# A first layer norm without a mean: centred embedding weights, squares summed on ScalarE

## The chip, the cores and the metric

The kernel runs on one core of one Trainium2 chip. The metric is the device time of one execution in microseconds (us). Of the kernel before there are three timed runs: 1298.17, 1299.24 and 1303.66 us, median 1299.24 us. The engines are called PE (TensorE), ACT (ScalarE), DVE (VectorE), POOL (GpSimd) and SP (the queue that starts most transfers).

## The reference

The model is an audio tower: patches of the signal are embedded and normalised, one attention layer follows, then a feed-forward layer in which each token picks 2 of 6 experts.

```
x: (128, 1000, 16)
patches = x[:, starts[:, None] + arange(16), :]      # stride 8: 124 tokens of 256 values
y   = einsum('bpi,di->bpd', patches, W) + b          # W 256 x 256
mu  = mean(y, axis=-1);  var = mean(square(y - mu), axis=-1)
h   = (y - mu) * rsqrt(var + 1e-5) * gamma + beta    # the first layer norm
h   = h + attention(layernorm(h))                    # one head of width 256, per batch item
h   = h + experts(layernorm(h))                      # router, softmax, top 2 of 6, 3-layer MLP each
```

The outputs are 128 x 124 tokens of 256 values in float32.

## The kernel before, in words

The kernel has two phases. The **first phase** takes 4 batch items (a group of 4 x 124 tokens) at a time, 32 groups in all, through a software pipeline. Every iteration `it` runs seven stages, each on another group: stage -2 splits the group's x into a rounded high part and a low part (`xT_hi` on ACT, `xT_lo` on DVE), stage -1 embeds it, stage 0 finishes the first layer norm and makes the second, stages 1 and 2 do attention, stages 3 and 4 the router, the choice of experts and the place of each token in its expert's list; stage 5 only sends the last rows. The loop runs `it` from -2 to 35. The **second phase** runs 67 tiles of 512 rows through the expert layers; two or three of its tiles are started between the last iterations of the first.

There is no scheduler: the order in which each engine takes its instructions is the order in which the code of its block is written, and engines wait for one another by counting semaphores. An instruction that waits holds back all that stands behind it on its engine. The semaphore `ln1` counts DVE's steps of one group in the first two layer norms (`LN1_N` of them), and `wait_apart` is a wait as an instruction of its own.

In stage -1 PE multiplies the group's patches by the embedding weights into banks 6 and 7 of PSUM, two batch items (a pair) per bank. The weights `proj_raw["tok"]` and the bias `bias_raw["tok"]` are split once at the start, high on ACT (`high_halves`, `high_bias`) and low on DVE (`low_halves`, `low_bias`). The product for the next group may overwrite a bank when DVE has made `y` from it (`bank_read`).

The steps that the change touches:

- DVE, stage -1, `statistics(0, ...)` (the line of `bn_stats` is L1030, that of `bn_aggr` L1033): for each of the four items a `bn_stats` over the 256 values of each token in PSUM, then an aggregation into mean and variance, `mv`.
- POOL, `inverse_std(0, ...)` (L499, L502): `rstd` of the group from the variance in `mv`. The same function serves the other two layer norms. Between its calls POOL issues eight indirect transfers (L510), which send each token's row to its experts' lists.
- DVE, stage -1, L1175: `y = (embedded - mean) * gamma`, four instructions, each of 256 columns.
- DVE, stage 0, L1098: `h = y * rstd + beta`; `statistics(1, ...)` for the second layer norm.
- ACT has no step between `xT_hi` (L905) and `qT` (L912).

Other names below: `half_w` (ACT L932, DVE L1143) is the splitting of the experts' weights, one piece of 256 columns in each iteration from 4 to 27 and three in each of 0 to 3; `nmr` (L1148, L1071) is minus mean times rstd of the second and third layer norm; `hav`, the residual sum behind attention, is L1161; `lshift` (L1235) is the router's logits less their maximum, which ACT's `pexp` (L858) reads; `rec` (L877) is the third layer norm's output, which PE transposes (L665); `xn` (L940) is the second's, transposed in L615.

Of the kernel before, what the change touches and what calls it, by code (L numbers as in the profile page):

```python
# [24 lines left out]
ALU = mybir.AluOpType  # L25
ACT = mybir.ActivationFunctionType
AX_X = mybir.AxisListType.X
# [34 lines left out]

LN1_N, AV_N, TOPK_N, POS_N = 25, 14, 25, 4
ADDED = 16 * TB
# [23 lines left out]
def audio_tower(nc, x, tok_w, tok_b, tok_gamma, tok_beta, wq, bq, wk, bk, wv, bv, scale,  # L88
                rw1, rb1, rw2, rb2, eweights, esmall, out):
    with ExitStack() as ctx:  # L90
# [36 lines left out]
        stats = sb("stats", [P, 3, GB, 6])  # L127
        mv = sb("mv", [P, 3, GB, 2])
        vareps = sb("vareps", [P, 3, GB])
        rstd = sb("rstd", [P, 3, GB])  # L130
# [42 lines left out]
        with ExitStack() as part_a:  # L173
# [30 lines left out]
        S = {n: sem(n) for n in (  # L204
            "tok_loaded", "const_loaded", "pool_const", "dve_const", "invs", "proj_high", "proj_low", "bias_zero",
            "w_high", "w_low", "dummy_cleared", "xT_high", "xT_low", "xn1T_low", "tok_ps", "ln1", "rstd1", "rstd2", "rstd3", "xn1_ready", "xn1T_ps", "xn1T_sb",
# [255 lines left out]
        def _(pool):  # L462
# [34 lines left out]
            def inverse_std(which, ready, g):  # L497

                pool.tensor_scalar(vareps[0:TOK, which, :], mv[0:TOK, which, :, 1], EPS, None,  # L499
                                   ALU.add).then_inc(ready, 1)  # L500
                pool.wait_ge(ready, g * 2 + 1)
                pool.tensor_tensor(rstd[0:TOK, which, :], vareps[0:TOK, which, :], neghalf[0:TOK, :],  # L502
                                   ALU.pow).then_inc(ready, 1)
# [10 lines left out]
            def step(it, group_of):  # L514
                xa, x0, x2, x4, x5 = (group_of(s) for s in (-1, 0, 2, 4, 5))
                if x0:
                    g, slot, rnd = x0
                    wait(pool, S["xn1_ready"], g * GB)
                    wait_apart(pool, S["ln1"], g * LN1_N + 6 * GB, S["pool_passed"])
                    inverse_std(1, S["rstd2"], g)  # L520
                if x5:
                    scatter(x5[0], range(5, 7))
                if xa:
                    g, slot, rnd = xa
                    wait_apart(pool, S["ln1"], g * LN1_N + 2 * GB, S["pool_passed"])
                    inverse_std(0, S["rstd1"], g)
                if x5:
                    scatter(x5[0], range(7, 8))
                if x2:
                    g, slot, rnd = x2  # L530
                    wait(pool, S["xn2_ready"], g * GB)
# [35 lines left out]
        def _(pe):  # L567
# [37 lines left out]
            def step(it, group_of):  # L605
# [21 lines left out]
                if it == DRAIN - 2:  # L627
                    pe.wait_ge(S["ln1"], (G - 1) * LN1_N + 3 * GB)
                    turn(0, 6)
# [8 lines left out]
                if xa:  # L638
                    g, slot, rnd = xa
                    pe.wait_ge(S["xT_high"], g + 1)  # L640
                    pe.wait_ge(S["xT_low"], g + 1)
                    if it == -1:
                        pe.wait_ge(S["proj_low"], 2)
                    for pair in range(2):
                        bank_read(pe, (S["ln1"], g - 1, (g - 1) * LN1_N + 2 * GB + 2 + 2 * pair))
                        for j in (0, 1):
                            at = (2 * pair + j) * ROWS_X
                            into = banks[6 + pair][0:TOK, j * D:(j + 1) * D]
                            for c in range(DC):
# [176 lines left out]
        def _(act):  # L826
# [20 lines left out]

            act.wait_ge(S["tok_loaded"], N_TOK)
            act.wait_ge(S["pool_const"], 2)
            high_halves("tok")  # L850
            high_bias("tok")

            def step(it, group_of):
                xs, x0, x1, x2, x3, x4 = (group_of(s) for s in (-2, 0, 1, 2, 3, 4))
                if x4:
# [44 lines left out]
                if xs:  # L900
# [3 lines left out]
                    wait(act, S["xT_low"], g)  # L904
                    act.activation(xT_hi[:], x_in[:, slot, :], ACT.Identity).then_inc(S["xT_high"], 1)  # L905
                if x1:
                    g, slot, rnd = x1
# [93 lines left out]
        def _(v):  # L1001
# [10 lines left out]

            v.wait_ge(S["tok_loaded"], N_TOK)
            v.wait_ge(S["pool_const"], 16)
# [3 lines left out]

            def embedded(j):

                return banks[6 + j // 2][R, (j % 2) * D:(j % 2 + 1) * D]

            def statistics(which, src, s, at, g):

                for j in range(GB):
                    if which == 0:
                        v.wait_ge(S["tok_ps"], g * 2 + j // 2 + 1)
                    else:
                        v.wait_ge(s, at - GB + 1 + j)
                    v.bn_stats(stats[R, which, j, :], src(j)).then_inc(s, 1)  # L1030
# [33 lines left out]
            def step(it, group_of):  # L1064
# [25 lines left out]
                if x0:  # L1090
# [5 lines left out]
                    for j in range(GB):  # L1096
                        v.wait_ge(S["ln1"], at + 2 * GB + 1 + j)
                        v.scalar_tensor_tensor(out=h[R, g % KEPT, j, :], in0=y[R, j, :], scalar=rstd[R, 0, j:j + 1],  # L1098
                                               in1=beta_bc[R, :], op0=ALU.mult, op1=ALU.add).then_inc(S["ln1"], 1)
                if x0:  # L1100
                    g, slot, rnd = x0
                    statistics(1, lambda j: h[R, g % KEPT, j, :], S["ln1"], g * LN1_N + 4 * GB, g)
                if x4:
# [46 lines left out]
                if it == DRAIN - 2:  # L1150
                    rows_low(0)
                if xa:
                    g, slot, rnd = xa
                    statistics(0, lambda j: embedded(j), S["ln1"], g * LN1_N, g)
                if x2:
# [270 lines left out]
```

## Time and profile before

| | |
|---|---|
| median of three timed runs | 1299.24 us |
| profiled execution: its own time, its span | 1298.97 us, 1297.2 us |
| PE, busy | 1222.9 us (94%) |
| PE weight loads, busy | 1075.9 us (83%) |
| DVE, busy | 1060.5 us (82%) |
| POOL, busy | 918.8 us (71%) |
| ACT, busy | 843.3 us (65%) |
| mean granted clock of PE | 0.984 |

The span is the time from the first to the last instruction; 1.8 us of the execution's own time lie around it. The shares are means over both phases. The first phase fills roughly the first 600 us, the second the rest, and the engines' shares differ between them. A row of the timeline gives start, duration (of a merged run of several instructions: from the first's start to the last's end), engine, line, operation, output and inputs, count, and in brackets how long the engine had been idle and what released it. Instructions of one engine overlap a little, so the distance from start to start is shorter than the duration.

### The profile page before, as it was taken

The page shows a single profiled execution, that of the slowest core. Times are in us where ns is not written, and L with a number is a line of the kernel's source. Part 1 is how long each engine was busy: PE and PEld are TensorE (multiplying, and loading weights), DVE is VectorE, ACT ScalarE, POOL GpSimd, SP SyncE. Part 2 cuts the span into 40 slices and gives each one's busy share as a digit, 9 for nine tenths or more (in the row PEclk, how much of TensorE's full clock was granted, in tenths as well). Part 3 has the DMA queues.
Part 4 walks back from the last instruction along what each step waited for, and adds up shares of the span by engine and source line. Part 5 has one row for each costly group of instructions (what it writes and reads, how often), then busy time and mean ns, then how long its engine had stood idle before and what let it go on. Part 6 is the DMA issues. An engine that isn't in the chain of part 4 may idle for free. (4 is left out here: it accounts for less than half of the span.)

```text
span 1297.2 us, 28243 instructions
## 1 busy us (share of the span) xinstructions
PE 1222.9 (94%) x7888; PEld 1075.9 (83%) x7888; DVE 1060.5 (82%) x3593; ACT 843.3 (65%) x1838; POOL 918.8 (71%) x740
## 2 busy tenths in 40 slices
PE   4999999999999999999898999999999999999993
PEld 4888888888888888888677888888888888889883
DVE  5789999999999999998777778777777777878783
ACT  2677677667667757776655667676666666666662
POOL 2127777877777777787788777777676767767776
PEclk8899999999999999999999999999999999999997
DMA  4224555544444444554469989766696687687745
GB/s 133 83 85 126 146 144 150 138 116 115 120 118 115 126 112 109 156 167 123 118 182 203 255 188 234 134 114 127 112 236 108 125 193 154 108 185 164 128 55 60
DMA packets 137193, 180.45 MB, mean 139 GB/s; under 512 B 38345, under 2 KB 103501, under 8 KB 137037
## 3 DMA queue, kind: packets, MB, share of 16 engines
q0 software_dynamic: 75456, 69.19, 32.9%
q1 hardware_dynamic: 60316, 108.67, 27.5%
q8 instruction: 64, 1.05, 0.3%
q10 hardware_dynamic: 1264, 0.79, 0.2%
q14 instruction: 93, 0.75, 0.2%
HBM read 159.01 MB, written 101.49 MB: 201 GB/s over the span
## 5 line engine op out<-in xcount | busy, mean ns | idle before, releaser
L559 POOL DMA_INDIRECT out<-yo,tail x268 | 434.2, 1620 | 168.8 <-issue 138.1
L510 POOL DMA_INDIRECT expert_rows<-rec,row_i x256 | 354.7, 1386 | 72.6 <-issue 59.4
L979 ACT ACTIVATE h2v<-bank,small 128x512 f32<-128x512 f32 x134 | 92.3, 690 | 204.6 <-PE bank L777 203.3
L804 PE MATMUL bank<-w_sb,h_hi 128*128 128x256 f32 x1072 | 208.8, 288 | 4.1 <-issue 3.6
L777 PE MATMUL bank<-x_hi,w_sb 128*128 128x512 f32 x536 | 178.6, 395 | 5.7 <-DVE x_lo L1337 4.8
L777 PE MATMUL bank<-h_hi,w_sb 128*128 128x512 f32 x536 | 177.4, 392 | 1.4 <-issue 1.4
L804 PEld LDWEIGHTS bank<-w_sb,h_hi 128*128 128x128 f32 x1072 | 171.6, 191 | 4.9 <-issue 4.2
L804 PE MATMUL bank<-w_sb,h_lo 128*128 128x256 f32 x536 | 151.7, 283 | 0.0
L777 PEld LDWEIGHTS bank<-x_hi,w_sb 128*128 128x128 f32 x536 | 101.8, 190 | 27.5 <-issue 5.0
L777 PEld LDWEIGHTS bank<-h_hi,w_sb 128*128 128x128 f32 x536 | 101.0, 188 | 21.4 <-issue 1.7
L985 ACT ACTIVATE yo<-yo,gcol 128x256 f32<-128x256 f32 x268 | 113.9, 498 | 4.7 <-DVE yo L1368 4.7
L573 PE MATMUL bank<-tok_proj,xT_hi 128*124 128x256 f32 x512 | 103.0, 294 | 13.6 <-DVE xT_lo L1139 9.4
L1352 DVE CAST h_hi<-h1v 128x512 fp32r<-128x512 f32 x134 | 62.4, 466 | 64.5 <-ACT h1v L972 64.5
L499 POOL TENSOR_SCALAR vareps<-mv 124x4 f32<-124x4 f32 x96 | 23.1, 241 | 123.5 <-issue 65.1
L502 POOL TENSOR_TENSOR rstd<-vareps,neghalf 124x4 f32<-124x4 f32 x96 | 102.4, 1067 | 8.0
L777 PE MATMUL bank<-x_lo,w_sb 128*128 128x512 f32 x268 | 105.4, 393 | 0.0
L777 PE MATMUL bank<-h_lo,w_sb 128*128 128x512 f32 x268 | 105.2, 392 | 0.0
L804 PEld LDWEIGHTS bank<-w_sb,h_lo 128*128 128x128 f32 x536 | 102.9, 192 | 0.0
L1352 DVE CAST h_hi<-h2v 128x512 fp32r<-128x512 f32 x134 | 58.1, 434 | 49.7 <-ACT h2v L979 49.4
L1337 DVE TENSOR_TENSOR h_lo<-h1v,h_hi 128x512 fp32r<-128x512 f32 x134 | 93.2, 695 | 4.6
L1337 DVE TENSOR_TENSOR h_lo<-h2v,h_hi 128x512 fp32r<-128x512 f32 x134 | 93.1, 694 | 4.6
L573 PE MATMUL bank<-v_proj,xn1T_hi 128*124 128x256 f32 x512 | 94.5, 285 | 0.0
(190 smaller groups left out, 3113.3 us busy)
## 6 DMA issues: line engine op xcount, KB each, us to landing
w_sb<-split_weights SPq DMA_DIRECT2D x189, 512.0 KB
xg<-expert_rows SPq DMA_DIRECT2D x67, 530.0 KB, 4.7
out<-h SPq DMA_DIRECT2D x32, 496.0 KB
split_weights<-half_w SPq DMA_DIRECT2D x36, 256.0 KB, 4.1
small<-in_esmall SPq DMA_DIRECT2D x67, 134.0 KB
x_in<-in_x SPq DMA_DIRECT2D x32, 250.0 KB, 10.7
expert_rows<-pad_rows SPq DMA_DIRECT2D x9, 530.0 KB, 9.1
raw_w<-in_eweights SPq DMA_DIRECT2D x36, 128.0 KB, 4.1
```

The source lines that it names most:

```text
L499: pool.tensor_scalar(vareps[0:TOK, which, :], mv[0:TOK, which, :, 1], EPS, None, ALU.add).then_inc(ready, 1)
L502: pool.tensor_tensor(rstd[0:TOK, which, :], vareps[0:TOK, which, :], neghalf[0:TOK, :], ALU.pow).then_inc(ready, 1)
L510: pool.indirect_dma_start(rows_dram, bass.IndirectOffsetOnAxis(ap=row_i[0:TOK, slot, j, k:k + 1], axis=0), rec[0:TOK, slot, j, :], None).t ...
L559: pool.indirect_dma_start(out, bass.IndirectOffsetOnAxis(ap=tail[:, t % TAILS, j, E8:].bitcast(I32), axis=0), yo[:, t % YO, j, :], None, c ...
L573: mm = pe.matmul(bank, lhs[a], rhs[b], start=(first and n == 0), stop=(last and n == 2))
L777: mm = pe.matmul(banks[bank + m][:], w[:, n, c, wh, m * P:(m + 1) * P], act[:, c, :], start=(c == 0 and p == 0), stop=(c == DC - 1 and p = ...
L804: mm = pe.matmul(banks[6 + b][:, (j % 2) * D:(j % 2 + 1) * D], act[:, c, j * P:(j + 1) * P], w[:, 2, c, wh, :], start=(c == 0 and p == 0), ...
L979: act.activation(h2v[:, m, :], banks[bank + m][:], ACT.Relu, bias=small[:, t % SLOTS, DC + m:DC + m + 1]).then_inc(S["h2_v"], 1)
L985: act.activation(yo[:, t % YO, j, :], yo[:, t % YO, j, :], ACT.Identity, scale=gcol[:, t % YO, j:j + 1]).then_inc(S["y_gated"], 1)
L1337: v.tensor_tensor(lo, val, hi.bitcast(F32), ALU.subtract).then_inc(ready, 1)
L1352: v.tensor_copy(hi[:, m, :], val[:, m, :]).then_inc(s, 1)
```

## The change

The embedding weights and the bias are made free of their mean over the 256 outputs, once, at the start, by DVE (`centre`). What PE then puts into PSUM has mean zero for each token, up to rounding. The mean is no longer computed or subtracted; the variance is the mean of the squares. ACT squares each item's 256 values from PSUM and lets the accumulator sum them into `sumsq`; POOL takes the variance from there. DVE's four `bn_stats` and four aggregations of the first layer norm go, and `y` is made by two instructions of 512 columns instead of four of 256. ACT's split of the embedding weights waits for `centre`.

```diff
-LN1_N, AV_N, TOPK_N, POS_N = 25, 14, 25, 4
+LN1_N, AV_N, TOPK_N, POS_N = 15, 14, 25, 4
...
             def inverse_std(which, ready, g):
-                pool.tensor_scalar(vareps[0:TOK, which, :], mv[0:TOK, which, :, 1], EPS, None,
-                                   ALU.add).then_inc(ready, 1)
+                if which == 0:
+                    pool.tensor_scalar(vareps[0:TOK, which, :], sumsq[0:TOK, :], 1.0 / D, EPS, ALU.mult,
+                                       ALU.add).then_inc(ready, 1)
+                else:
+                    pool.tensor_scalar(vareps[0:TOK, which, :], mv[0:TOK, which, :, 1], EPS, None,
+                                       ALU.add).then_inc(ready, 1)
...
                 if xa:
                     g, slot, rnd = xa
-                    wait_apart(pool, S["ln1"], g * LN1_N + 2 * GB, S["pool_passed"])
+                    wait_apart(pool, S["squares"], (g + 1) * GB, S["pool_passed"])
                     inverse_std(0, S["rstd1"], g)
...
-                        bank_read(pe, (S["ln1"], g - 1, (g - 1) * LN1_N + 2 * GB + 2 + 2 * pair))
+                        bank_read(pe, (S["ln1"], g - 1, (g - 1) * LN1_N + 1 + pair))
...
-            act.wait_ge(S["tok_loaded"], N_TOK)
+            act.wait_ge(S["centred"], 4)
             act.wait_ge(S["pool_const"], 2)
             high_halves("tok")
+            act.wait_ge(S["centred"], 10)
             high_bias("tok")
...
+                if xa:
+                    g, slot, rnd = xa
+                    wait(act, S["rstd1"], g * 2)
+                    for j in range(GB):
+                        act.wait_ge(S["tok_ps"], g * 2 + j // 2 + 1)
+                        wait(act, S["squares"], g * GB + j)
+                        act.activation(square[0:TOK, :], banks[6 + j // 2][0:TOK, (j % 2) * D:(j % 2 + 1) * D], ACT.Square,
+                                       accum_out=sumsq[0:TOK, j:j + 1]).then_inc(S["squares"], 1)
...
+            def centre():
+
+                s = S["centred"]
+                v.wait_ge(S["tok_loaded"], N_TOK)
+                v.tensor_reduce(tok_mean[:], proj_raw["tok"][:], AX_X, ALU.add).then_inc(s, 1)
+                v.wait_ge(s, 1)
+                v.tensor_scalar(tok_mean[:], tok_mean[:], 1.0 / D, None, ALU.mult).then_inc(s, 1)
+                v.wait_ge(s, 2)
+                for c in range(DC):
+                    v.tensor_scalar(proj_raw["tok"][:, c, :], proj_raw["tok"][:, c, :], tok_mean[:, c:c + 1], None,
+                                    ALU.subtract).then_inc(s, 1)
...
+            centre()
             v.wait_ge(S["pool_const"], 16)
             low_halves("tok", 1)
             low_bias("tok", 3)
...
-                if xa:
-                    g, slot, rnd = xa
-                    statistics(0, lambda j: embedded(j), S["ln1"], g * LN1_N, g)
...
-                    for j in range(GB):
-                        v.wait_ge(S["ln1"], at + GB + 1 + j)
-                        v.scalar_tensor_tensor(out=y[R, j, :], in0=embedded(j), scalar=mv[R, 0, j, 0:1],
-                                               in1=gamma_bc[R, :], op0=ALU.subtract, op1=ALU.mult).then_inc(S["ln1"], 1)
+                    for pair in range(2):
+                        v.wait_ge(S["squares"], g * GB + 2 * pair + 2)
+                        v.tensor_tensor(y[R, 2 * pair:2 * pair + 2, :],
+                                        banks[6 + pair][R, :].rearrange("p (b n) -> p b n", b=2),
+                                        gamma_bc[R, :].unsqueeze(1).to_broadcast([TOK, 2, D]), ALU.mult
+                                        ).then_inc(S["ln1"], 1)
```

The part left out of `centre` does the same with the bias: for its copies in partitions 0 and 32 a sum over the 256 values, a product with 1/256 and a subtraction.

DVE, from the weights' split to the router's shift, in one steady iteration before:

```order
L1143 TENSOR_TENSOR half_w<-raw_w,half_w 128x256
L1148 SCALAR_TENSOR_TENSOR nmr<-mv,rstd 124x4
L1030 BN_STATS stats<-bank 124x6 x4
L1033 BN_AGGR mv<-stats 124x2 x4
L1161 SCALAR_TENSOR_TENSOR h<-bank,rinv,h 124x256 x4
L1030 BN_STATS stats<-h 124x6 x4
L1033 BN_AGGR mv<-stats 124x2 x4
L1175 SCALAR_TENSOR_TENSOR y<-bank,mv,gamma_bc 124x256 x4
L1230 TENSOR_TENSOR logits<-bank,rb_bc 124x4x6
L1233 TENSOR_REDUCE lmax<-logits 124x4
L1235 TENSOR_TENSOR lshift<-logits,lmax 124x32
```

The same stretch of DVE now:

```order
L1173 TENSOR_TENSOR half_w<-raw_w,half_w 128x256
L1178 SCALAR_TENSOR_TENSOR nmr<-mv,rstd 124x4
L1188 SCALAR_TENSOR_TENSOR h<-bank,rinv,h 124x256 x4
L1060 BN_STATS stats<-h 124x6 x4
L1063 BN_AGGR mv<-stats 124x2 x4
L1202 TENSOR_TENSOR y<-bank,gamma_bc 124x512 x2
L1259 TENSOR_TENSOR logits<-bank,rb_bc 124x4x6
L1262 TENSOR_REDUCE lmax<-logits 124x4
L1264 TENSOR_TENSOR lshift<-logits,lmax 124x32
```

The statistics of the bank are gone, and `h`, which reads PE's attention output, follows `nmr` at once; `y` is two instructions.

ACT, from the router's exponential on, in one steady iteration before:

```order
L858 ACTIVATE pexp<-lshift 124x32
L866 ACTIVATE xn1T<-bank,ones_r 128x496 x2
L870 ACTIVATE xn1T_hi<-xn1T 128x496 x2
L877 ACTIVATE rec<-h,nmr,rstd 124x256 x4
L886 ACTIVATE probs<-bank,negmax 124x124 x4
L893 ACTIVATE xn2T<-bank 128x496 x2
L899 ACTIVATE gexp<-gap 124x4
L905 ACTIVATE xT_hi<-x_in 128x500
L912 ACTIVATE qT<-bank,score_col 128x496 x2
L917 ACTIVATE pT<-bank 125x496
L921 ACTIVATE rhT<-bank,rb_col 128x496
L932 ACTIVATE half_w<-raw_w 128x256
```

The same stretch of ACT now:

```order
L866 ACTIVATE pexp<-lshift 124x32
L874 ACTIVATE xn1T<-bank,ones_r 128x496 x2
L878 ACTIVATE xn1T_hi<-xn1T 128x496 x2
L885 ACTIVATE rec<-h,nmr,rstd 124x256 x4
L894 ACTIVATE probs<-bank,negmax 124x124 x4
L901 ACTIVATE xn2T<-bank 128x496 x2
L907 ACTIVATE gexp<-gap 124x4
L913 ACTIVATE xT_hi<-x_in 128x500
L920 ACTIVATE square,sumsq<-bank 124x256 x4
L928 ACTIVATE qT<-bank,score_col 128x496 x2
L933 ACTIVATE pT<-bank 125x496
L937 ACTIVATE rhT<-bank,rb_col 128x496
```

Four squares stand between `xT_hi` and `qT`, ahead of `pT`, `rhT` and `half_w`. On PE nothing moves; on POOL the second `rstd` of an iteration waits for `squares` instead of `ln1`.

## Rows read from the trace of the kernel before

**Rows 1.** One iteration: length, busy PE, PEld, DVE, ACT, POOL (instructions), clock, DMA.
```profile
309.90:328.90 19.00, 18.31 (x130) 15.95 (x129) 17.39 (x79) 13.32 (x32) 14.92 (x15) 1.00 0.45 118
```
**Rows 2.** Timeline of DVE: `negmax` of the iterations 4 and 28.
```profile
85.74 0.67 DVE L1076 TENSOR_REDUCE negmax<-bank 124x4 f32<-124x496 f32 x1
...
543.81 0.67 DVE L1076 TENSOR_REDUCE negmax<-bank 124x4 f32<-124x496 f32 x1
```
**Rows 3.** Timeline of DVE, second half of one iteration.
```profile
323.87 0.43 DVE L1143 TENSOR_TENSOR half_w<-raw_w,half_w 128x256 fp32r<-128x256 f32 x1 [0.57 <-ACT half_w L932]
...
324.28 1.42 DVE L1030 BATCH_NORM_STATS2 stats<-bank 124x6 f32<-124x256 f32 x4
...
325.97 1.66 DVE L1161 SCALAR_TENSOR_TENSOR h<-bank,rinv,h 124x256 f32<-124x256 f32 x4
...
329.18 1.63 DVE L1175 SCALAR_TENSOR_TENSOR y<-bank,mv,gamma_bc 124x256 f32<-124x256 f32 x4
330.73 0.17 DVE L1230 TENSOR_TENSOR logits<-bank,rb_bc 124x24 f32<-124x24 f32 x1
...
331.15 0.19 DVE L1235 TENSOR_TENSOR lshift<-logits,lmax 124x32 f32<-124x32 f32 x1
```
**Rows 4.** Timeline of ACT, from `pexp` of that iteration to its `rhT`.
```profile
312.39 0.23 ACT L858 ACTIVATE pexp<-lshift 124x32 f32<-124x32 f32 x1 [2.51 <-DVE lshift L1235]
312.52 1.22 ACT L866 ACTIVATE xn1T<-bank,ones_r 128x496 f32<-128x496 f32 x2
...
321.19 0.58 ACT L917 ACTIVATE pT<-bank 125x496 f32<-125x496 f32 x1 [0.27 <-PE bank L700]
322.86 0.67 ACT L921 ACTIVATE rhT<-bank,rb_col 128x496 f32<-128x496 f32 x1 [1.09 <-PE bank L708]
```
**Rows 5.** Timeline of PE in the same iteration.
```profile
314.86 0.28 PE L652 MATMUL bank<-tok_bias,ones_r 128*124 128x256 f32 x1
315.39 0.73 PE L665 MATMUL bank<-ident,rec 124*128 124x124 f32 x2 [0.26 <-ACT rec L877]
...
317.28 0.47 PE L573 MATMUL bank<-xn1T_hi,q_proj 128*128 128x496 f32 x1
...
322.65 1.89 PE L722 MATMUL bank<-v_sb,pT 125*124 125x256 f32 x8
...
328.08 1.01 PE L615 MATMUL bank<-ident,xn 124*128 124x124 f32 x8
```
**Rows 6.** Timeline of POOL: the same transfer in two iterations that follow one another.
```profile
552.50 1.43 POOL L510 DMA_INDIRECT expert_rows<-rec,row_i  x1 [0.24 <-issue]
...
570.09 1.43 POOL L510 DMA_INDIRECT expert_rows<-rec,row_i  x1 [0.24 <-issue]
```
**Rows 7.** Timeline of ACT: `probs`, with the read of its accumulator.
```profile
297.63 0.35 ACT L886 ACTIVATE probs<-bank,negmax 124x124 f32<-124x124 f32 x1
297.87 0.20 ACT L886 ACTIVATION_READ_ACCUMULATOR probs<-bank,negmax 124x1 f32 x1
297.97 0.35 ACT L886 ACTIVATE probs<-bank,negmax 124x124 f32<-124x124 f32 x1
```
**Rows 8.** Groups by line; columns: count | busy us, mean ns | idle before.
```profile
L1368 DVE TENSOR_TENSOR yo<-bank,small 128x512 f32<-128x512 f32 x134 | 85.8, 681 | 2.2 <-PE bank L804 2.2
...
L940 ACT ACTIVATE xn<-h,nmr,rstd 124x256 f32<-124x256 f32 x128 | 66.4, 590 | 18.2 <-DVE nmr L1148 18.2
...
L952 ACT ACTIVATE v_sb<-bank 124x512 f32<-124x512 f32 x64 | 37.9, 596 | 38.8 <-PE bank L573 38.8
...
L932 ACT ACTIVATE half_w<-raw_w 128x256 fp32r<-128x256 f32 x36 | 13.8, 407 | 0.0
...
L840 ACT ACT_TABLE_LOAD x1 | 1.3, 1283 | 4.4 <-POOL pad_rows L489 4.4
...
L1039 DVE TENSOR_REDUCE key_sum<-bank 128x2 f32<-128x512 f32 x1 | 0.7, 674 | 0.0
```
**Rows 9.** Timeline of DVE: its first instruction.
```profile
7.18 0.69 DVE L1005 TENSOR_TENSOR tok_proj<-tok_raw,tok_proj 128x512 fp32r<-128x512 f32 x1 [7.18 <-ACT tok_proj L840]
```

More of the change, by code:

```diff
@@ L128, in audio_tower @@
         mv = sb("mv", [P, 3, GB, 2])
+        square = sb("square", [P, D])
+        sumsq = sb("sumsq", [P, GB])
+        tok_mean, bias_mean = sb("tok_mean", [P, DC]), sb("bias_mean", [P, 1])
         vareps = sb("vareps", [P, 3, GB])
@@ L204, in audio_tower @@
         S = {n: sem(n) for n in (
-            "tok_loaded", "const_loaded", "pool_const", "dve_const", "invs", "proj_high", "proj_low", "bias_zero",
+            "tok_loaded", "const_loaded", "centred", "squares", "pool_const", "dve_const", "invs", "proj_high", "proj_low", "bias_zero",
             "w_high", "w_low", "dummy_cleared", "xT_high", "xT_low", "xn1T_low", "tok_ps", "ln1", "rstd1", "rstd2", "rstd3", "xn1_ready", "xn1T_ps", "xn1T_sb",
@@ L518, in step @@
                     wait(pool, S["xn1_ready"], g * GB)
-                    wait_apart(pool, S["ln1"], g * LN1_N + 6 * GB, S["pool_passed"])
+                    wait_apart(pool, S["ln1"], g * LN1_N + 2 + 3 * GB, S["pool_passed"])
                     inverse_std(1, S["rstd2"], g)
@@ L627, in step @@
                 if it == DRAIN - 2:
-                    pe.wait_ge(S["ln1"], (G - 1) * LN1_N + 3 * GB)
+                    pe.wait_ge(S["ln1"], (G - 1) * LN1_N + 2)
                     turn(0, 6)
@@ L846, in high_bias @@
                                    ).then_inc(S["proj_high"], 1)
-            act.wait_ge(S["tok_loaded"], N_TOK)
+            act.wait_ge(S["centred"], 4)
             act.wait_ge(S["pool_const"], 2)
             high_halves("tok")
+            act.wait_ge(S["centred"], 10)
             high_bias("tok")
             def step(it, group_of):
-                xs, x0, x1, x2, x3, x4 = (group_of(s) for s in (-2, 0, 1, 2, 3, 4))
+                xs, xa, x0, x1, x2, x3, x4 = (group_of(s) for s in range(-2, DEPTH))
                 if x4:
@@ L1011, in low_bias @@
                                 ALU.subtract).then_inc(S["proj_low"], 1)
-            v.wait_ge(S["tok_loaded"], N_TOK)
+            def centre():
[8 more added lines that the diff above has]
+                                    ALU.subtract).then_inc(s, 1)
+                for r in (0, 32):
+                    v.tensor_reduce(bias_mean[r:r + 1, :], bias_raw["tok"][r:r + 1, :], AX_X, ALU.add).then_inc(s, 1)
+                v.wait_ge(s, 6)
+                for r in (0, 32):
+                    v.tensor_scalar(bias_mean[r:r + 1, :], bias_mean[r:r + 1, :], 1.0 / D, None, ALU.mult).then_inc(s, 1)
+                v.wait_ge(s, 8)
+                for r in (0, 32):
+                    v.tensor_scalar(bias_raw["tok"][r:r + 1, :], bias_raw["tok"][r:r + 1, :], bias_mean[r:r + 1, 0:1], None,
+                                    ALU.subtract).then_inc(s, 1)
+            centre()
             v.wait_ge(S["pool_const"], 16)
@@ L1017, in _ @@
             R = slice(0, TOK)
-            def embedded(j):
-                return banks[6 + j // 2][R, (j % 2) * D:(j % 2 + 1) * D]
             def statistics(which, src, s, at, g):
                 for j in range(GB):
[L1026 to L1029, printed above, removed]
+                    v.wait_ge(s, at - GB + 1 + j)
                     v.bn_stats(stats[R, which, j, :], src(j)).then_inc(s, 1)
@@ L1096, in step @@
                     for j in range(GB):
-                        v.wait_ge(S["ln1"], at + 2 * GB + 1 + j)
+                        v.wait_ge(S["ln1"], at + 1 + j // 2)
                         v.scalar_tensor_tensor(out=h[R, g % KEPT, j, :], in0=y[R, j, :], scalar=rstd[R, 0, j:j + 1],
@@ L1101, in step @@
                     g, slot, rnd = x0
-                    statistics(1, lambda j: h[R, g % KEPT, j, :], S["ln1"], g * LN1_N + 4 * GB, g)
+                    statistics(1, lambda j: h[R, g % KEPT, j, :], S["ln1"], g * LN1_N + 2 + GB, g)
                 if x4:
```

## Prediction, made before the changed kernel ran

> **What bounds the kernel now.** I read the busy time by stretch first, then the timelines of the engines through one iteration, then the single forms. The change touches only the first phase and the start, so the second phase is taken as it is.
>
> One steady iteration of the first phase takes 19.0 us; in it PE is busy for 18.3, DVE 17.4, POOL 14.9 and ACT 13.3 us, at a full granted clock [rows 1]. The `negmax` of iterations 4 and 28 stand 458.07 us apart, 24 iterations of 19.09 us; 2.1 us of these are extras, 1.7 of them the choice of the early expert in one iteration [rows 2]. No busy share says which engine sets the 19.0 us, so I followed the waits round one turn:
>
> - DVE waits 0.57 us for ACT's `half_w` at 323.87 us and then runs until `lshift` ends at 331.34 us: 7.47 us [rows 3].
> - `lshift` releases ACT's `pexp`, for which ACT had idled 2.51 us. From `pexp` at 312.39 us ACT goes through its list to the `half_w` that releases DVE at 323.87 us: 11.48 us. Within them ACT idles 0.27 us ahead of `pT` and 1.09 ahead of `rhT`, for PE [rows 3, 4].
>
> 7.47 + 11.48 + 0.03 for the handover = 18.98 us: this ring is the bound, DVE for two fifths of it, then ACT and PE.
>
> Just below it lie the engines alone. PE idles 0.41 us ahead of its transposes of `rec` (314.86 + 0.12 to 315.39 us), which then take 1.89 us, paced by ACT, where eight of the same form in L615 take 1.01 us to the last end, some 0.85 to the next start: 19.0 - 0.41 - 1.04 = 17.55 us [rows 5]. POOL, where it waits for nobody, needs 17.59 us for a turn [rows 6]. DVE, less its 0.57 us and some 0.5 of smaller waits, needs about 17.9.
>
> **The change, part by part.**
>
> *DVE, the statistics.* From the bank's `bn_stats` at 324.28 us to L1161 at 325.97 us: 1.69 us go [rows 3]. They lie on the ring.
>
> *DVE, `y`.* Four instructions take 1.55 us from start to start (329.18 to 330.73 us) [rows 3]. The two new ones have the form of L1368, 512 columns from a bank with a broadcast operand, 0.68 us each [rows 8]; start to start some 0.61. 1.55 - 1.22 = 0.33 us go, also on the ring. It would be 0.19 if they did not overlap.
>
> *ACT, four squares.* The trace has no square. A plain pass over 512 columns of a bank takes 0.596 us, a plain one over 256 columns of SBUF 0.407 [rows 8]; I take 0.42 for 256 from a bank. The accumulator's read follows: in `probs` it begins 0.24 us after the start of a 0.35 us pass, lasts 0.20 and so ends 0.09 us behind it [rows 7]. Each square waits for the one before, with another 0.03: 0.42 + 0.09 + 0.03 = 0.54, say 0.53 us each and 2.1 us for the four. Lower bound: `probs` repeats every 0.34 us [rows 7] and 132 more columns add 0.11: 0.45, in all 1.8. Upper bound: as slow as L940's 0.590 us pass with two pointer operands [rows 8] and the same 0.12: 0.71, in all 2.8.
>
> The page "ScalarE: Activation LUTs" of the Trainium skill, section "What ACT_TABLE_LOAD costs", gives a pass with immediate operands as 186 ns plus 0.833 ns per column, 399 ns here, and 93 ns for each pointer operand; L932's 407 ns and L940's 590 ns agree. By it a square is 0.52 us, the four 2.1; with a pointer as bias it would be 0.61 and 2.45.
>
> On the ring the squares stand ahead of `pT` and `rhT`. They first fill the 1.36 us for which ACT idles there, and lengthen ACT's part only by 2.1 - 1.36 = 0.74 us.
>
> *The new ring.* 18.98 - 1.69 - 0.33 + 0.74 = 17.7 us. A second one comes up beside it. ACT from `xn1T` at 312.52 to the end of `pT` at 321.77 us is 9.25 us, less the 0.27 idle, plus the squares: 11.1 us. The late `pT` holds back PE's L722, and from there (322.65 us) to the end of the transposes of `xn` (329.09 us) are 6.44 us, upon which ACT's `xn1T` waits: 17.5 us [rows 4, 5]. With PE's 17.55 and POOL's 17.59 four limits lie within 0.2 us. I take 17.75 us for the iteration, a little above the highest.
>
> *POOL.* Its `rstd1` will find the squares done long before (they end some 9 us behind `pexp`), so that one wait goes. It was not on the ring. In iterations 28 to 30, where there is no `half_w`, the period is set by DVE alone before (17.6 to 17.9) and by the second ring now: no gain.
>
> *What is queued behind the new waits.* Behind the squares on ACT stand `qT`, `pT`, `rhT` and `half_w`, and PE and DVE wait for these; this is counted above. DVE's `y` waits for the squares, which end some 7 us before its turn. Its `h` (L1161) now comes 1.69 us earlier after `nmr`, but DVE's 0.57 us wait for `half_w` grows to about 1.4, so it arrives when PE's product is there.
>
> *The start.* DVE's first work was at 7.18 us, behind ACT's split [rows 9]. Now `centre` comes ahead of ACT: a reduction over 512 columns (0.67 us as L1039 [rows 8]), a small product, two subtractions; then the bias, four passes over 256 columns of one partition and two small ones. That is 3 to 4 us of DVE, partly beside ACT's split; PE's first product starts about 2.6 us later. In the first iterations PE's product, two squares and `y` form a chain, 1.1 us of squares in place of 1.7 of statistics, while three `half_w` stand behind the squares. I count +2 us until iteration 3 (bounds 0 and +4).
>
> **The sum.** 24 iterations of 17.75 us are 426.0 us. Of the 2.1 us of extras I leave 1.0, since the longer wait of DVE at `half_w` covers part of the early choice: 427. 458.07 - 427 = 31 us saved. Iteration 3 to 4 gives 1 more, the start costs 2: 30 us. The execution profiled took 1298.97 us, which is 0.3 below the median, so no correction: 1298.97 - 30 = **1269 us**. Its own range goes by the squares: at 1.8 us the other limits hold 17.6, saving 33 to 34; at 2.45 the ring is 18.1, saving some 22: 1264 to 1278.
>
> **The rivals.**
>
> *ACT takes the ring over.* Squares at 2.8 us make 18.4 us an iteration: 24 x 0.6 = 14 us saved and 1 from the extras, less the start: about 1285. For it: four serial steps, each with an accumulator read, on the engine whose slack ahead of `pT` is only 1.36 us. Against it: ACT is busy 13.3 of 19 us and the forms nearest are short. The page named above says in "Rules for kernel authors" that plain multiplications belong on VectorE rather than on ScalarE, which speaks against this move; the row of L932 against the 1.69 us on DVE shows that ACT's price is higher, 2.1 against 1.7, but paid in idle time.
>
> *PE is the bound already.* If its 18.31 busy of 19.0 us could not be compressed, an iteration would stay at 18.4 or more: 24 x 0.6 = 15 us, less 2: again about 1285. Against it speaks that its transposes of `rec` take twice the time of the same ones of `xn` [rows 5].
>
> *The time goes up.* ACT has one load of its function table, 1.28 us, at the start [rows 8]. If `Square` is not held beside `Exp`, each iteration has two more, 2.57 us, on the ring: the squares' block costs 4.7 us, the ring is 20.3 us, 24 x 1.2 = 29 us lost and some more at both ends: about 1330. It turns slower where the block exceeds 1.36 + 2.02 = 3.4 us. Against it: the changed program still has a single table load among ACT's instructions, ahead of the loop. The page's section "Table sets: the hidden batching unit" says that cheap functions stand in every set, and gives 2.66 us for a switch; by that the loss would be twice as large.
>
> *The change does not take effect*, because the mean or the squares would be needed twice: nothing in the code does so; no chance of its own.
>
> **Chances.** Forecast (1262 to 1279) 0.72; ACT's ring at 18.2 to 18.8 us 0.13; PE bound 0.08; slower by the tables or a longer start than thought 0.04; a cause that I do not see and that eats the gain 0.03. The range for 8 in 10 is 1261 to 1283: it takes in the forecast and the nearer part of the two rivals. What a measurement can tell from no change is 0.5%, 6.5 us: faster 0.92, same 0.04, slower 0.04.
>
> **What would show it.** In the changed profile: `negmax` of iterations 4 and 28 about 427 us apart; a square of about 0.38 to 0.44 us with a read of 0.20 behind it, 0.5 to 0.55 from start to start; DVE's wait ahead of L1173 (`half_w` low) grown from 0.57 to some 1.4 us and ACT's wait ahead of `pexp` shrunk from 2.5 to under 1; no wait of ACT ahead of `pT`; POOL without a wait ahead of `rstd1`; PE's waits for `rec` nearly gone; its first product at about 12 us. The prediction is wrong if the squares repeat at over 0.65 us, if a table load shows in the loop, or if a wait of PE or DVE that I do not name holds the iteration above 18.2 us.

## The result and the profile after

The changed kernel takes 1259.5 us (median of four runs, 1257.0 to 1265.5), the kernel before 1298.7 us beside it: ratio 0.970, 95% interval 0.9685 to 0.972. A second series of five runs gave 1259.9 us against 1298.4, ratio 0.970 (0.9686 to 0.9717). The prediction was 1269 us with 1261 to 1283: the direction and the mechanism hold, but the gain is some 39 us where 30 were forecast, and the time lies 1 to 1.5 us below the range.

One profiled execution of the changed kernel has a span of 1263.7 us, the one of the second series 1260.1. The first one's extra time is made before iteration 4 and between the phases; its loop is the same. The rows below are of the first unless said otherwise.

The page, busy time over the span. VectorE (DVE) has 62 us less than before, ScalarE (ACT) 51 more:
```profile
PE 1207.0 (96%) x7888; PEld 1073.8 (85%) x7888; DVE 998.4 (79%) x3283; ACT 894.7 (71%) x2094; POOL 918.5 (73%) x740
```
Two successive iterations of the first phase, by stretch (the columns of [rows 1]). They last 35.28 us, 17.64 each, where one took 19.00:
```profile
296.53:331.81 35.28, 35.28 (x259) 31.56 (x258) 30.82 (x134) 29.85 (x81) 29.92 (x29) 1.00 0.51 129
```
DVE's timeline, `negmax` of the iterations 4, 28 and 33, then one iteration. The first two answer to [rows 2] and stand 424.26 us apart (424.13 in the second series), not 458.07. The rest answers to [rows 3]: DVE waits 1.15 us for `half_w` (0.57 before), the bank's statistics are gone, and from `half_w` to the end of `lshift` it needs 308.63 to 314.05 = 5.42 us (7.47 before):
```profile
86.32 0.67 DVE L1106 TENSOR_REDUCE negmax<-bank 124x4 f32<-124x496 f32 x1
...
510.58 0.67 DVE L1106 TENSOR_REDUCE negmax<-bank 124x4 f32<-124x496 f32 x1
...
597.75 0.67 DVE L1106 TENSOR_REDUCE negmax<-bank 124x4 f32<-124x496 f32 x1
...
308.63 0.42 DVE L1173 TENSOR_TENSOR half_w<-raw_w,half_w 128x256 fp32r<-128x256 f32 x1 [1.15 <-ACT half_w L948]
...
312.25 1.26 DVE L1202 TENSOR_TENSOR y<-bank,gamma_bc 124x512 f32<-124x512 f32 x2
313.43 0.17 DVE L1259 TENSOR_TENSOR logits<-bank,rb_bc 124x24 f32<-124x24 f32 x1
...
313.86 0.19 DVE L1264 TENSOR_TENSOR lshift<-logits,lmax 124x32 f32<-124x32 f32 x1
...
326.31 0.42 DVE L1173 TENSOR_TENSOR half_w<-raw_w,half_w 128x256 fp32r<-128x256 f32 x1 [1.12 <-ACT half_w L948]
```
ACT's timeline of the same iteration answers to [rows 4]. Its wait ahead of `pexp` is 0.41 and 0.25 us (2.51 before). A square begins every 0.56 to 0.58 us, and the four take 303.66 to 305.75 = 2.09 us. `qT`'s two passes then take 1.23 us, and `pT` starts without a wait:
```profile
296.53 0.23 ACT L866 ACTIVATE pexp<-lshift 124x32 f32<-124x32 f32 x1 [0.41 <-DVE lshift L1264]
...
303.66 0.40 ACT L920 ACTIVATE square<-bank 124x256 f32<-124x256 f32 x1
303.92 0.23 ACT L920 ACTIVATION_READ_ACCUMULATOR square<-bank 124x1 f32 x1
304.24 0.39 ACT L920 ACTIVATE square<-bank 124x256 f32<-124x256 f32 x1
...
305.75 1.23 ACT L928 ACTIVATE qT<-bank,score_col 128x496 f32<-128x496 f32 x2
306.86 0.59 ACT L933 ACTIVATE pT<-bank 125x496 f32<-125x496 f32 x1
307.62 0.67 ACT L937 ACTIVATE rhT<-bank,rb_col 128x496 f32<-128x496 f32 x1 [0.16 <-PE bank L715]
308.19 0.41 ACT L948 ACTIVATE half_w<-raw_w 128x256 fp32r<-128x256 f32 x1
...
314.08 0.23 ACT L866 ACTIVATE pexp<-lshift 124x32 f32<-124x32 f32 x1 [0.25 <-DVE lshift L1264]
```
PE's timeline, to [rows 5]: the transposes of `rec` follow the last bias product without a gap and take 301.22 to 301.99 = 0.77 us up to the next product, where they took 1.89:
```profile
301.11 0.28 PE L659 MATMUL bank<-tok_bias,ones_r 128*124 128x256 f32 x1
301.22 1.01 PE L672 MATMUL bank<-ident,rec 124*128 124x124 f32 x8
301.99 0.48 PE L580 MATMUL bank<-xn1T_hi,q_proj 128*128 128x496 f32 x1
...
307.51 1.99 PE L729 MATMUL bank<-v_sb,pT 125*124 125x256 f32 x8
```
Where the time went, from `negmax` in the profiled executions of before and of the second series (they differ by 37.1 us in the span):

| stretch | before | after | saved | forecast |
|---|---|---|---|---|
| start to iteration 4 | 85.74 | 85.23 | 0.5 | -1 |
| iterations 4 to 28 | 458.07 | 424.13 | 33.9 | 31 |
| iterations 28 to 33 | 89.88 | 87.18 | 2.7 | 0 |
| the rest | 663.5 | 663.6 | 0 | 0 |

The forecast's sum missed 7.1 us here: 1.5, 2.9 and 2.7. The other 2 us are the difference between this execution's own time, 1261.9 us, and the median.

### The profile page after: what moved, and what is told of

The parts are those of the page before. It is cut to its first block, busy times and chain, and to the rows that moved or that the text cites. A ratio compares the mean times of both kernels' runs of the same rounds, so it can differ in the third digit from the quotient of the medians.

```text
span 1263.7 us, 28188 instructions
## 1 busy us (share of the span) xinstructions
PE 1207.0 (96%) x7888; PEld 1073.8 (85%) x7888; DVE 998.4 (79%) x3283; ACT 894.7 (71%) x2094; POOL 918.5 (73%) x740
## 4 chain that ended last, share of the span: by engine, by line
PE 86%; DVE 5%; ACT 4%; issue 3%; POOL 1%; DMA 0%; POOLq 0%; SPq 0%; ACTq 0%; DVEq 0%
PE bank L784 29%; PE bank L580 18%; PE bank L811 15%; PE bank L773 4%; PE bank L729 4%; PE bank L715 4%; PE bank L631 4%; PE bank L622 2%; PE bank L672 2%; PE bank L737 2%; PE bank L707 1%; PE bank L659 1%; ACT rec L885 1%; ACT square L920 1%; DVE h L1188 1%
## 5 line engine op out<-in xcount | busy, mean ns | idle before, releaser
L517 POOL DMA_INDIRECT expert_rows<-rec,row_i x256 | 358.5, 1401 | 72.8 <-issue 61.0
L580 PE MATMUL bank<-tok_proj,xT_hi 128*124 128x256 f32 x512 | 103.9, 296 | 14.9 <-DVE xT_lo L1169 12.3
L580 PEld LDWEIGHTS bank<-tok_proj,xT_hi 128*124 128x124 f32 x512 | 81.5, 195 | 15.0 <-issue 15.0
```

What stands on the lines that cost most here:

```text
L517: pool.indirect_dma_start(rows_dram, bass.IndirectOffsetOnAxis(ap=row_i[0:TOK, slot, j, k:k + 1], axis=0), rec[0:TOK, slot, j, :], None).t ...
L580: mm = pe.matmul(bank, lhs[a], rhs[b], start=(first and n == 0), stop=(last and n == 2))
```

## The experiments

Theory: before, the ring of DVE and ACT set the iteration; the squares lie mostly in ACT's idle time, and after the change the ring, PE's own work and GpSimd's (POOL's) own chain are nearly level. The rivals were ACT as the new bound, and PE or POOL as a floor that makes the squares free.

**The changed kernel again**, as the base of the others.

> The changed kernel once more, to see how much of the 39 us between the medians belongs to every run. In its first trace iterations 4 to 28 took 424.3 us and the third tile of the second phase came 16.9 us behind the second, where 10.1 us stood before; ACT waited 8.6 us there for a transfer of small. Theory: the long gap is chance in a transfer, and the trace of a run near 1258 us shows again 424 us for the 24 iterations and a third tile about 10 us behind the second. Rival: the gap belongs to the change, and this trace has it too, with a time near 1265 us.

Measured: 1259.9 us, ratio 0.970 (0.9686 to 0.9717), the table above; 24 iterations take 424.13 us. ACT's wait for a transfer of `small`, 8.58 us at 662.02 us of the first execution, does not come again, which speaks for chance in a transfer, as expected.

**The centring alone**, in the kernel before.
```diff
+            centre()          # the changed kernel's, and ACT's two waits for it
             v.wait_ge(S["pool_const"], 16)
             low_halves("tok", 1)
```


> The kernel before with centre alone: the embedding weights and the bias are centred at the start, while the statistics, the subtraction of the mean and everything behind them stay. Theory: PE's first product starts about 2 us later and all later stages shift by as much, some 2 us slower, 24 iterations unchanged at 458 us. Rival: the start is covered by later waits, no difference.

Measured: 1301.9 us, +3.6 where some 2 were expected; ratio 1.0028 (1.0017 to 1.0038). Its loop is the old one (458.14 us for 24 iterations), so all of it is the start: `negmax` of iteration 4 comes at 90.52 us, 4.8 later. PE's first product is only 2.7 us late (12.12 against 9.4 us). The other 2 us are added while PE works, 1.1 of them in the first group. PE's products of the second group begin 3.8 us later, those behind its next long wait (36.97 against 32.55 us) 4.4, the transposes of `xn` (52.31 against 47.57 us) 4.7. Before, the later products of the first group took 0.39 us a pair:
```profile
13.12 0.39 PE L573 MATMUL bank<-tok_proj,xT_hi 128*124 128x256 f32 x2
...
18.62 0.76 PE L573 MATMUL bank<-tok_proj,xT_hi 128*124 128x256 f32 x2 [4.04 <-DVE y L1175]
```
With the centring alone they take 0.63 us until the end, as those in the stretches of low clock do, although the granted clock is 1.00 in the rows:
```profile
15.88 0.63 PE L574 MATMUL bank<-tok_proj,xT_hi 128*124 128x256 f32 x2
...
22.40 0.76 PE L574 MATMUL bank<-tok_proj,xT_hi 128*124 128x256 f32 x2 [4.04 <-DVE y L1198]
```
In the next two groups both kernels have a stretch at a lower clock; PE works through 4.7 and 7.8 us of it before, and through 6.0 and 8.5 with the centring. By stretch before, when the low clock is over:
```profile
24.00:28.00 4.00, 4.00 (x29) 3.53 (x28) 3.02 (x10) 2.76 (x7) 0.14 (x1) 1.00 0.24 78
```
and with the centring alone, when it is not:
```profile
24.00:28.00 4.00, 4.00 (x21) 4.00 (x20) 2.37 (x10) 0.00 (x0) 1.27 (x2) 0.50 0.00 0
```
A granted clock (third column from the right) of 0.50 is the level of 1.2 GHz. That the lower pace makes the 2 us is worked out from these rows; no run varied it. What the whole change then wins back in its first iterations is more than these 4.8 us.

**The squares left out**, in the changed kernel; a constant stands for their sum, so the first norm's scale is left out.
```diff
-                    for j in range(GB):
-                        ...
-                        act.activation(square[...], ..., ACT.Square, accum_out=sumsq[...])
...
+            pool.memset(sumsq[:], 80.0)
```


> The changed kernel without the four squares of an iteration on ACT: the sums are a constant, so the first layer norm scales by a constant. Theory: ACT's squares are paid for by ACT's idle time, and POOL and PE alone already need 17.5 to 17.6 us for an iteration, so the 24 iterations take 421 to 424 us, as with the squares; only the start gets shorter by 1 to 2 us: 2 to 4 us faster than the changed kernel. Rival: the ring through ACT sets the 17.68 us; without its 2.1 us the iteration falls to 17.0 or less, 16 us or more faster than the changed kernel.

Measured: 1253.7 us, ratio 0.9648 (0.9632 to 0.9665). 24 iterations take 420.87 us, 3.3 less than with the squares; a steady one 17.53 us instead of 17.63. The whole is 6.2 us below the changed kernel's, more than the 2 to 4 expected: 2.5 us of it are gained before iteration 4, and 2.4 between the profiled executions lie behind the loop. By stretch, one iteration: PE is busy in all of it.
```profile
302.00:319.53 17.53, 17.53 (x130) 15.88 (x129) 15.32 (x67) 13.34 (x32) 14.84 (x15) 1.00 0.48 130
```
So the squares, 2.09 us of ACT's time in an iteration, cost the kernel 0.10 us of it: the rest was paid in idle time. PE's own work, forecast at 17.55 us, is the floor. The full busy time does not show that, for the changed kernel's two iterations above have it too, at 17.64 us. The distances from start to start do: on PE all are the same in both kernels but those of the product with `pT` (1.73 us here, 1.75 to 1.83 in the changed kernel) and of the one ahead of it (1.67 against 1.67 to 1.76).

**The squares added** to the kernel before, whose statistics on DVE stay and wait for the squares of their bank.
```diff
+                        act.activation(square[...], ..., ACT.Square, accum_out=sumsq[...])
...
-                        v.wait_ge(S["tok_ps"], g * 2 + j // 2 + 1)
+                        v.wait_ge(S["squares"], g * GB + j // 2 * 2 + 2)
```


> The kernel before with the four squares added on ACT at the place they have in the changed kernel, their sums unused; DVE's statistics of a bank wait for the squares of that bank, since two engines may not read one bank at once. Theory: before the change the ring through ACT and DVE sets the iteration; the squares' 2.1 us fill 1.36 us of ACT's idle time and lengthen the ring by 0.7: 19.6 to 19.8 us for an iteration, 24 iterations in some 474 us, 17 to 20 us slower than before. Rival 1: hidden altogether, 458 us. Rival 2: paid in full, 21.1 us for an iteration, 50 us slower.

Measured: 1307.4 us, ratio 1.0069 (1.0054 to 1.0085). An iteration takes 19.33 us against 19.00: 2.09 us of squares lengthen the ring by 0.33, not by 0.74, and the 24 iterations by 7.5 us where 17 to 20 were expected. ACT's timeline of it:
```profile
300.82 0.23 ACT L860 ACTIVATE pexp<-lshift 124x32 f32<-124x32 f32 x1 [2.04 <-DVE lshift L1245]
...
307.94 0.40 ACT L914 ACTIVATE square<-bank 124x256 f32<-124x256 f32 x1
...
310.02 1.23 ACT L922 ACTIVATE qT<-bank,score_col 128x496 f32<-128x496 f32 x2
311.14 0.59 ACT L927 ACTIVATE pT<-bank 125x496 f32<-125x496 f32 x1
311.60 0.69 ACT L931 ACTIVATE rhT<-bank,rb_col 128x496 f32<-128x496 f32 x1
```
DVE's `half_w` follows at 312.63 us: 11.81 us from `pexp`, 11.48 before. The slack was therefore about 2.09 - 0.33 = 1.76 us, where the brackets of [rows 4] add up to 1.36. Two things were missing in that sum. Unhindered, `pT` starts 0.46 us ahead of `rhT` here, and thus 0.1 us before its own end; a bracket counts only from the end. And `qT`'s pair takes 1.23 us here, when before it took 1.42, with idle time inside a merged row.

**The squares behind `half_w`** and ahead of `xn`, in the changed kernel.
```diff
-                if xa:    # ahead of qT, pT, rhT and half_w
-                    ...squares...
...
+                if xa:    # behind half_w
+                    ...squares...
```


> The changed kernel with ACT's four squares moved behind half_w and ahead of xn. Without squares an iteration took 17.53 us, with them 17.68. Theory: the 0.15 us come from the squares' place ahead of pT, which PE waits for; moved, they fill ACT's idle time ahead of xn and v_sb, and the iteration falls to the 17.53 us that POOL or PE sets: 24 iterations in 421 us, 2 to 4 us faster than the changed kernel. Rival: the difference is the squares' mere presence (bank reads, later rstd1), no gain, 424 us.

Measured: 1258.8 us (1255.0 to 1259.6), ratio 0.9685 (0.9667 to 0.9702). By the trace 24 iterations take 420.51 us, 3.6 less than in the second series, and a steady one 17.53 us, as with no squares at all. The groups of PE's weight loads by line show what the place ahead of `pT` costs. In the changed kernel, over 371 us:
```profile
L729 PEld LDWEIGHTS bank<-v_sb,pT 125*124 125x124 f32 x168 | 29.7, 186 | 18.0 <-ACT pT L933 14.4
```
and with the late squares:
```profile
L729 PEld LDWEIGHTS bank<-v_sb,pT 125*124 125x124 f32 x170 | 31.7, 187 | 13.7 <-issue 10.0
```
The wait for `pT` is gone, and the idle time ahead of these loads falls by 4.3 us. Over the whole kernel the intervals of this version and of the changed one overlap, so that it is faster stands on the loop's 3.6 us alone; it has the lowest median of all versions that compute everything.

**POOL shortened:** the additions of epsilon of the second and third norm go to DVE.
```diff
-                    pool.tensor_scalar(vareps[0:TOK, which, :], mv[0:TOK, which, :, 1], EPS, None, ALU.add)
...
+                v.tensor_scalar(vareps[R, which, :], mv[R, which, :, 1], EPS, None, ALU.add)
```


> The changed kernel with 0.6 us less on POOL in each iteration: the addition of epsilon for the second and third layer norm runs on DVE behind the aggregation, so POOL keeps its eight transfers, three powers and one addition. Theory A: POOL, which never waits in the changed kernel, sets the iteration; it falls by up to 0.2 us, until PE and the ring through ACT hold it near 17.5. Theory B: PE sets it; POOL only waits more and the iteration stays at 17.6 to 17.7 us.

Measured: 1267.7 us, ratio 0.976 (0.974 to 0.9781); an iteration 17.75 us. POOL now waits ahead of the second norm's `rstd`, by the code for DVE's sum, which ends at 307.91 us. Its timeline, that operation in two successive iterations, with the idle time in brackets:
```profile
308.08 1.04 POOL L506 TENSOR_TENSOR rstd<-vareps,neghalf 124x4 f32<-124x4 f32 x1 [0.83 <-issue]
...
326.17 1.04 POOL L506 TENSOR_TENSOR rstd<-vareps,neghalf 124x4 f32<-124x4 f32 x1 [1.23 <-issue]
```
So POOL was not the limit. DVE's small additions lie on the ring, whose DVE part is 311.42 to 317.06 = 5.64 us now, 0.22 more than in the changed kernel. The iteration grew by 0.12: with `rhT` waiting for PE and PE for `pT`, it lies above both the ring's own length, 17.5 us, and PE's 17.53. One iteration takes 20.06 us, and the medians differ by 7.7 us where the loop and iterations 28 to 33 give 5.5; neither that iteration nor the rest is explained.

**PE shortened:** the embedding's bias product is left out of the changed kernel.
```diff
-                            mm = pe.matmul(into, ones_r[:, 0:TOK], bias_row["tok"][:], start=False, stop=True)
```


> The changed kernel without the bias product of the embedding, four products of 0.12 us and their weight loads in each iteration: the embedding's bias is left out. Theory A (POOL sets the iteration): PE waits 0.5 us more and the iteration stays at 17.6 us. Theory B (PE sets it): 24 iterations take 11 us less, 413 us. Where both are limits of almost the same height, neither this run nor the one with a shorter POOL gains more than 0.2 us an iteration.

Measured: 1254.7 us, ratio 0.9664 (0.965 to 0.9678); 24 iterations 419.30 us, 4.8 less, and most steady ones 17.40 or 17.41 us. PE lost 0.47 us an iteration and the kernel 0.20: a next limit is close, as the expectation's last sentence allowed for. The last experiment shows which.

**Each square twice**, in the changed kernel.
```diff
+                        for again in (0, 1):
                             ...
                             act.activation(square[...], ..., ACT.Square, accum_out=sumsq[...])
```


> The changed kernel with each square made twice, eight on ACT in an iteration, 2.1 us more. Theory: the ring DVE half_w, lshift, ACT pexp to half_w measures 5.4 + 11.8 = 17.2 us in the changed kernel, below the 17.68 us of the iteration; 2.3 us more ACT makes it 19.3 to 19.6, 24 iterations in 463 to 470 us, some 40 us slower than the changed kernel. Rival: ACT's idle time takes half of it, 18.5 us.

Measured: 1353.6 us, ratio 1.0421 (1.0404 to 1.0437). An undisturbed iteration takes 19.70 us: 2.07 more than 17.63. The 24 iterations take 491.6 us where 463 to 470 were expected, since many of them take 21.4 or 22.9 us; the last section has their rows. The 2.07 us are a sum. Without a wait the ring of the changed kernel is 17.27 us: 10.33 from `pexp` to `pT`, 0.46 to `rhT`, 1.03 to DVE's `half_w`, 5.42 to the end of `lshift`, 0.03 to `pexp`. Eight squares take 4.34 us instead of 2.09, 2.25 more. And ACT's `xn2T`, which reads PE's transposes of `rec`, starts 0.18 us later behind `probs` than in the changed kernel: 17.27 + 2.25 + 0.18 = 19.70. So the slack is used up, and beyond it ACT's time counts in full; that the 2.07 us so nearly equal the 2.09 of four squares is chance.

**`y` as four products** of 256 columns, in the changed kernel.
```diff
-                    for pair in range(2):
-                        ...v.tensor_tensor(y[R, 2 * pair:2 * pair + 2, :], ..., ALU.mult)
+                    for j in range(GB):
+                        ...v.tensor_tensor(y[R, j, :], ..., gamma_bc[R, :], ALU.mult)
```


> The changed kernel with the first norm's product y written as four products of 256 columns again (without the subtraction), where it has two of 512. Two products took 1.28 us from start to start of what follows, the four of the kernel before 1.61 us with their subtraction: the four should take 1.45 to 1.65 us. Theory (the ring of VectorE and ScalarE sets the iteration of 17.68 us, with TensorE's own 17.53 us close behind): VectorE's 0.2 to 0.35 us go into the iteration, which becomes 17.85 to 18.0 us, and the time 1264 to 1269 us. Rival (TensorE or GpSimd sets the iteration and VectorE has 0.3 us to spare): the iteration stays at 17.68 us within 0.05 us, the time within 2 us of the changed kernel's 1260 us.

Measured: 1261.7 us, ratio 0.9725 (0.9712 to 0.9739), 24 iterations 425.07 us. The timeline of DVE:
```profile
312.39 1.39 DVE L1202 TENSOR_TENSOR y<-bank,gamma_bc 124x256 f32<-124x256 f32 x4
```
1.39 us against 1.26 with two products and 1.63 before: most of what `y` saves comes from the missing subtraction. The 0.13 us made the iteration 0.04 us longer, so the expected 17.85 to 18.0 us failed, first by the size of the edit, then because the ring has some room under PE's limit: an iteration of 17.87 us is followed by one of 17.53.

**Late squares and no bias product.**

> The changed kernel with the squares behind half_w, and without the embedding's bias product on TensorE (so its output leaves out the embedding's bias). The squares' move alone gave 17.53 us an iteration with TensorE busy throughout, the bias product's removal alone 17.47 us; the product takes TensorE 0.47 us. Theory A (GpSimd's own chain of indirect transfers and powers is the next limit, at some 17.4 us): the iteration is 17.35 to 17.45 us, and the time 1250 to 1253 us. Theory B (only the ring, shortened by both, and TensorE count): it is 17.1 to 17.3 us, and the time 1244 to 1250 us.

Measured: 1254.0 us, ratio 0.9673 (0.966 to 0.9687); an iteration of 17.42 us, inside theory A's interval, while the time is 1 us above its. PE alone would allow 17.53 - 0.47 = 17.06. POOL's timeline from one transfer to the same one a turn later, 301.57 to 318.98 = 17.41 us, names no wait for another engine:
```profile
301.57 1.42 POOL L517 DMA_INDIRECT expert_rows<-rec,row_i  x1 [0.24 <-issue]
303.30 1.32 POOL L517 DMA_INDIRECT expert_rows<-rec,row_i  x1 [0.30 <-issue]
304.69 0.19 POOL L503 TENSOR_SCALAR vareps<-sumsq 124x4 f32<-124x4 f32 x1
304.96 1.04 POOL L509 TENSOR_TENSOR rstd<-vareps,neghalf 124x4 f32<-124x4 f32 x1
...
311.08 1.32 POOL L517 DMA_INDIRECT expert_rows<-rec,row_i  x1 [0.30 <-issue]
...
317.70 1.05 POOL L509 TENSOR_TENSOR rstd<-vareps,neghalf 124x4 f32<-124x4 f32 x1
318.98 1.42 POOL L517 DMA_INDIRECT expert_rows<-rec,row_i  x1 [0.24 <-issue]
```
The brackets alone do not show that POOL is the limit, for in the changed kernel they look the same in turns of 17.6 to 17.7 us. What differs is how long a transfer lasts. In the changed kernel one of them is stretched:
```profile
317.32 1.54 POOL L517 DMA_INDIRECT expert_rows<-rec,row_i  x1 [0.30 <-issue]
```
Here that transfer takes 1.32 us, like the shortest of all, and so it does in the kernel without the bias product, where a turn takes 17.40. So POOL is the next limit, 0.11 us under PE. PE's length shows in iterations 4 and 5 of this run, 17.13 and 17.05 us, in which POOL still waits, the last time 0.61 us for a square. [rows 6] had put POOL at 17.59; a turn in that place has a transfer of 1.55 us.

## Why the prediction was right or wrong

- **The ring was the bound: right.** DVE's part shrank by 7.47 - 5.42 = 2.05 us, forecast 1.69 + 0.33 = 2.02.
- **The four squares at 2.1 us: right.** 2.09 us, the pass 0.389 us in the mean and the accumulator's read 0.20. The page "ScalarE: Activation LUTs" of the Trainium skill, section "What ACT_TABLE_LOAD costs", gives 399 ns for such a pass; the trace agrees. No table load stands in the loop, only the one of 1.28 us ahead of it, so the rival on the far side is out. The 2.66 us for a switch that the prediction cites stand in that section of the page and not in the one that it names; no run here shows a switch.
- **"They lengthen ACT's part only by 2.1 - 1.36 = 0.74 us": the size was wrong.** It is 0.33 us, by the kernel with the squares added. The idle brackets understate the slack of a paced engine: 1.36 us where it was 1.76. The ring alone comes to 19.33 - 2.02 = 17.3 us, and not to 17.7; 17.27 is also the sum of its parts without waits. In the changed kernel itself `rhT` still waits 0.16 to 0.29 us for PE, so this length is worked out and not seen.
- **PE's own 17.55 us: right.** 17.53, by the two kernels without squares ahead of `pT`. The other 0.10 us of the changed kernel's iteration are PE's wait for `pT` and its slower restart behind it.
- **"I take 17.75 us for the iteration, a little above the highest": the step that failed first.** It is 17.63 us. The highest of the four limits stood on the 1.36 us; without that error it would have been POOL's 17.59, itself too high (17.42, by the last experiment), with PE's 17.55 below it. 24 x 0.12 = 2.9 us of the miss. The extras of 1.0 us hold: 424.13 - 24 x 17.63 = 1.0.
- **"In iterations 28 to 30 ... no gain", carried on to 33: wrong by 2.7 us.** 2.2 of them are one iteration of 19.31 us that became 17.13. Before, PE idled in it and then ran at a lower clock; the last section has the rows. The other three went from 17.85, 17.75 and 17.58 to 17.62, 17.49 and 17.53 us: DVE alone set them, as said, and DVE is what the change relieves. The forecast put a second ring at 17.5 in its place and then counted nothing for the difference.
- **"I count +2 us until iteration 3", and +1 of gain after it: wrong by 1.5 us.** The first product came at 12.1 to 12.3 us, as forecast, and the centring costs even 3.6 to 4.8 us by itself. But the other half of the change gives back more than all of it by iteration 4: from the kernel with the centring alone to the changed one 90.52 - 85.23 = 5.3 us, in iterations where DVE has the most to do.
- **The range.** The three errors have one sign: the iteration was set above every limit, and start and end were counted as a loss and as nothing. For the lower end only the squares were varied, and the other three terms held still; 33 to 34 us saved plus the 3 to 4 us of start and end give the 37 that came.
- **The rivals.** ACT's ring at 18.2 us or more and PE's bound at 18.4 are refuted: 17.63 us. That PE is the floor is true, only at 17.53; its 18.31 busy microseconds of before held stretched transposes, as [rows 5] said.

## What to carry to other kernels

Work moved onto an engine that waits in the middle of a ring is nearly free up to its slack and costs time beyond it (2.09 us of squares cost 0.33 us an iteration in the kernel before and 0.10 in the changed one; 2.25 us more cost 2.07). The slack is to be read as the distance from where the engine would start unhindered to where it did, over its whole list, also inside merged rows; the brackets give less. And when several small terms are each set on the careful side, the range has to reach as far as all of them together.

## What the runs showed of the hardware

A wait of PE can cost more than its length, as the granted clock falls after it, but not each time. In the kernel with each square twice PE waits 1.9 to 2.2 us for `pT` in every steady iteration. PE's timeline, that product in two successive ones:
```profile
192.53 3.05 PE L729 MATMUL bank<-v_sb,pT 125*124 125x256 f32 x8 [1.91 <-ACT pT L934]
...
215.44 1.99 PE L729 MATMUL bank<-v_sb,pT 125*124 125x256 f32 x8 [1.94 <-ACT pT L934]
```
and the two iterations by stretch, 22.91 us at a mean clock of 0.85, and 19.70 us at 1.00:
```profile
181.14:204.05 22.91, 21.00 (x130) 18.65 (x129) 15.68 (x67) 16.76 (x49) 16.93 (x16) 0.85 0.55 145
204.05:223.75 19.70, 17.76 (x130) 15.78 (x129) 15.02 (x68) 16.68 (x49) 13.11 (x14) 1.00 0.44 119
```
The same happened once in the kernel before, in the iteration of 19.31 us. PE's timeline and the stretches after it:
```profile
598.60 0.73 PE L665 MATMUL bank<-ident,rec 124*128 124x124 f32 x2 [1.24 <-ACT rec L877]
```
```profile
599.00:601.00 2.00, 1.67 (x8) 1.30 (x9) 1.93 (x12) 2.00 (x9) 1.70 (x2) 0.78 0.32 84
601.00:603.00 2.00, 2.00 (x6) 1.64 (x6) 2.00 (x7) 1.34 (x5) 1.63 (x2) 0.50 0.57 167
603.00:605.00 2.00, 2.00 (x12) 1.60 (x10) 1.40 (x12) 0.67 (x1) 1.64 (x3) 0.86 0.48 128
```
After the change the clock of that iteration is 1.00. With the squares added to the kernel before it was 17.7 us long too, although nothing had been taken off DVE there, so this 1.6 to 2.2 us need not come from the work removed. Why one such wait lowers the clock and the next of the same length doesn't stays open.
